# Order of the squared states between ScalarE and TensorE in a Mamba + MoE kernel: by batch, or by row

## What is computed

```
def step(h, inp):
    dA_t, dB_t, x_t, C_t, t = inp
    h = h * dA_t + dB_t * x_t[:, :, None]
    nrm = jnp.sqrt(jnp.sum(h * h, axis=(1, 2), keepdims=True))
    fac = jnp.minimum(20.0 / (nrm + 1e-08), 1.0)
    h = jnp.where(t % 10 == 0, h * fac, h)
    y = jnp.einsum('bdn,bn->bd', h, C_t) + D_param * x_t
    return (h, y)
```

## Time and profile before

| | us |
|---|---|
| runs of the kernel before | 733.01, 736.2, 736.84 |
| median of them | 736.2 |
| span of the profiled execution | 732.8 |
| PE / PE weight loads busy | 610.7 / 475.9 |
| DVE / ACT / POOL busy | 579.2 / 581.7 / 591.9 |
| segments run from | about 36 to 600 |

### The profile page before, as it was taken

How to read it: one execution, slowest core, us unless ns; L and a number is a source line. 1 busy time by engine, 2 the same in 40 slices (tenths; PEclk the granted TensorE clock), 3 DMA queues, 4 the chain that set the end, 5 groups by cost and what they waited for, 6 DMA issues and landing times.

```text
span 732.8 us, 12812 instructions
## 1 busy us (share of the span) xinstructions
PE 610.7 (83%) x3988; PEld 475.9 (65%) x3988; DVE 579.2 (79%) x918; ACT 581.7 (79%) x1218; POOL 591.9 (81%) x567
## 2 busy tenths in 40 slices
PE   6698989889979889998988999898878794289774
PEld 4346667757757667766766766776667783179764
DVE  5577799899889989998998999889898982843221
ACT  4899989999998999999999999999988731233330
POOL 4488889999998989999998999998798860177774
PEclk9889899999989999999999999999988887589998
DMA  5341423245145313614542271244215202147561
GB/s 159 117 157 36 146 80 117 62 143 162 61 145 144 127 63 100 202 61 133 156 127 63 85 210 64 105 139 133 64 66 175 66 18 73 47 129 207 167 182 48
DMA packets 61735, 83.17 MB, mean 114 GB/s; under 512 B 14998, under 2 KB 47544, under 8 KB 61672
## 3 DMA queue, kind: packets, MB, share of 16 engines
q1 hardware_dynamic: 57896, 76.07, 34.0%
q0 software_dynamic: 2560, 6.08, 3.0%
q10 hardware_dynamic: 1216, 0.27, 0.2%
HBM read 69.81 MB, written 12.80 MB: 113 GB/s over the span
## 4 chain that ended last, share of the span: by engine, by line
ACT 27%; PE 22%; issue 17%; POOL 15%; DVE 13%; DMA 4%; POOLq 0%; SPq 0%; DVEq 0%; ACTq 0%
ACT z L1098 9%; POOL h L855 8%; DVE h L1367 7%; PE ps L1725 7%; ACT ps L989 7%; POOL h L869 4%; PE ps L1617 4%; DMA z<-rows_d,gidx 3%; PE ps L588 2%; PE ps L601 2%; ACT L1059 2%; ACT dtb L1059 1%; ACT xx L1016 1%; PE ps L1699 1%; ACT L1098 1%
## 5 line engine op out<-in xcount | busy, mean ns | idle before, releaser
L1367 DVE TENSOR_TENSOR_SCAN h<-ps,h 128x902 f32<-128x902 f32 x204 | 320.4, 1610 | 33.5 <-ACT ps L989 23.6
L855 POOL TENSOR_TENSOR h<-u,scr 128x640 f32<-128x640 f32 x208 | 298.2, 1462 | 2.4
L1725 PEld LDWEIGHTS ps<-h,ident 128*128 128x128 f32 x1632 | 239.4, 199 | 24.2 <-issue 21.8
L1725 PE MATMUL ps<-h,ident 128*128 128x160 f32 x1632 | 243.9, 310 | 3.3 <-issue 3.3
L1098 ACT ACTIVATE z<-dtb,asc 128x240 f32<-128x240 f32 x576 | 237.4, 485 | 0.3
L989 ACT ACTIVATE ps<-z 128x820 f32<-128x820 f32 (+1 forms) x208 | 138.2, 689 | 16.0 <-DVE h L1367 8.9
L869 POOL TENSOR_TENSOR h<-h,scr 128x960 f32<-128x960 f32 (+1 forms) x52 | 106.0, 2038 | 1.1 <-DVE h L1383 1.1
L1418 DVE TENSOR_TENSOR h<-h,ps 128x640 f32<-128x640 f32 (+2 forms) x169 | 106.5, 642 | 0.2
L1617 PE MATMUL ps<-xnT,wT 128*128 128x488 f32 x144 | 77.2, 652 | 0.3 <-ACT xnT L974 0.3
L1699 PE MATMUL ps<-sqb,sel 128*8 128x32 f32 x832 | 33.6, 195 | 37.6 <-ACT sqb L999 27.7
L1699 PEld LDWEIGHTS ps<-sqb,sel 128*8 128x8 f32 x832 | 27.2, 91 | 53.0 <-ACT sqb L999 45.7
(11 more groups left out here) (193 smaller groups left out, 820.2 us busy)
## 6 DMA issues: line engine op xcount, KB each, us to landing
scr<-b_d SPq DMA_DIRECT2D x52, 640.0 KB, 4.6
scr<-c_d SPq DMA_DIRECT2D x52, 240.0 KB, 4.4
z<-in_L_ffn_w_dram SPq DMA_DIRECT2D x32, 256.0 KB, 3.1
cdg<-cdg_d SPq DMA_DIRECT2D x52, 93.8 KB, 2.1
xx_d<-xx SPq DMA_DIRECT2D x8, 256.0 KB, 2.0
xxr<-xx_d SPq DMA_DIRECT2D x8, 256.0 KB, 2.8
rows_d<-h2b SPq DMA_DIRECT2D x16, 120.0 KB, 2.0
rows_d<-xxr SPq DMA_DIRECT2D x16, 120.0 KB, 2.3
```

The lines of the kernel that those rows point to most:

```text
L855: pool.tensor_tensor(o.rearrange("p (n b) t -> p n b t", b=B), us.unsqueeze(1).to_broadcast([P, nn, B, SEG]), bb[:, S % RING, n0 * BS:(n0 ...
L1367: dve.tensor_tensor_scan(hs, region(G)[:, 0:(r1 - r0) * SLOT], hs, 0.0, ALU.mult, ALU.add).then_inc(gscan, 1)
L1725: pe.matmul(ps[:, YB, 0:H * BS], ident[:], hr[:, :, n * B:(n + 1) * B, 0:SEG], start=(n == 0), stop=False)
```

## The change

The squares are written in the order of the rows, so that the output of ACT (and of DVE in the one operation ahead of the first segment) is contiguous; PE then takes a batch's 32 values with a stride of eight, 32 bytes apart. No instruction is added, removed or moved on any engine; only the addresses of three kinds of operation differ.

```diff
+        sq_b = sqb[:].rearrange("p (r b) -> p b r", b=B)
...
                 r0, r1 = ((0, SQROW), (SQROW, ROWS))[part]
-                act.activation(sqb[:].rearrange("p (b r) -> p r b", b=B)[:, r0 // B:r1 // B, :],
-                               rows(h, S % RING)[:, r0:r1, SEG].rearrange("p (r b) -> p r b", b=B),
+                act.activation(sqb[:, r0:r1], rows(h, S % RING)[:, r0:r1, SEG],
                                ACT.Square).then_inc(sq_done, 1)
...
-            dve.tensor_tensor(sqb[:].rearrange("p (b r) -> p r b", b=B), h_first.rearrange("p (r b) -> p r b", b=B),
-                              h_first.rearrange("p (r b) -> p r b", b=B), ALU.mult).then_inc(sq_done, 1)
+            dve.tensor_tensor(sqb[:], h_first, h_first, ALU.mult).then_inc(sq_done, 1)
...
                 for b in range(B):
-                    ins = pe.matmul(ps[0:B, YB, NCOL:NCOL + H * NST], sel[:, b, :], sqb[:, b * H * NST:(b + 1) * H * NST],
+                    ins = pe.matmul(ps[0:B, YB, NCOL:NCOL + H * NST], sel[:, b, :], sq_b[:, b, :],
                                     start=(b == 0), stop=(b == B - 1))
```

## The result

The changed kernel takes 746.1 us (744.28 to 747.95, four runs) against 735.11 us (733.01 to 736.84, four runs): ratio 1.0158, 95% interval 1.0123 to 1.0194. It is slower by 11.0 us, 1.6%. The profiled execution took 745.95 us, with a span of 744.2 us against 732.8.

What follows compares the result with a forecast made beforehand. No engine bounds the span; the norm chain ends last at a segment's end. PE's 0.43 us a norm, less covers, gives 1.26 us a window, 10.5 in all, other terms 0: 736.2 to 746.7 us, range 733.5 to 751.

Steps and rivals of the forecast that it cites:

- The bound: At each segment's end, PE's norm chain ends last by 0.10 us, so time added to PE delays DVE's reduction.
- (a): ACT's squares: contiguous output with input still strided changes nothing; taken as 0, at most 0.05 us a segment.
- The argument from DVE: DVE's squares: strided input alone costs 2.06 ns a value, both sides 1.90, contiguous runs 1.06; strided output adds nothing.
- (c): PE's norm, 16 matmuls reading values 32 bytes apart: 0.43 us more a segment, between 0 and 0.62.
- The factor of two: PE's columns in the norm: a strided value doubles the price, as on ACT and DVE, 0.85 ns extra.
- The covers: Waits behind the norm, DVE's for ACT's decays and POOL's late start, absorb part; 1.26 us a six-segment window is paid.
- The waits of 0.35 and 0.36 us: DVE's scans waiting for ACT's decays behind two norms of a window; they leave 0.08 and 0.07 us of 0.43 paid.
- The sum: Whole kernel: 1.26 us a window over 8.3 windows, 10.5 us more, median 736.2 to 746.7; chance 0.46.
- PE's cadence hides the stride: Rival on PE's norm: the 0.85 ns float32 column hides the stride; 734.5 to 736.2 us, chance 0.39.
- A partial price: Rival on PE's norm: 0.1 to 0.3 us a norm; at 0.3, 6 us more, 742; chance 0.08.
- DVE's full price: Rival on PE's norm: 0.62 us a norm, 18.3 us more, 754.5; chance 0.04.
- the output was ACT's cost: Rival on ACT's squares: contiguous output shortens them to 376 and 238 ns; at most 1.7 us gained; chance 0.03, including anything faster.

Runs made afterwards that it cites:

- bf16_rows: Changed kernel with squares in bf16, in the order of the rows, PE's stride of eight being 16 bytes; 743.84 us against 734.19 (ratio 1.0129).
- stride three: Kernel before, PE taking its 32 values with a stride of three (12 bytes); one run, 748.5 us, where the kernel before took 750.17 us.
- stride four: Kernel before, PE taking its 32 values with a stride of four (16 bytes), each on its own line; ratio 1.0155.
- act_only: Changed kernel with PE's line put back to reading neighbours, leaving the output order alone; 732.54 us against 734.32 (ratio 0.9979).

## Why the prediction was right, point by point

- **The bound** was read rightly: the norm chain ended last by a tenth of a microsecond, and DVE's stand before `take_norm` rose from 0.10 to 0.58 us, by PE's extra time. That not all of it is paid had been said too; how much is absorbed is where the sizes went wrong.
- **(a)** Taken at 0, right within 10 and 2 ns an operation. The argument from DVE (a strided input alone doubles the price) was tested on ACT: input alone 574, output alone 574, both 584, neither 372 ns. I had drawn the value of neither at 376.
- **(c)** Sized at 0.43 us a norm, it is 0.49. The factor of two was the right form only by accident of the numbers. The runs show a pace of about one line in 1.8 ns, not a doubled column: bf16 columns, at half the price, are slowed to the same 58 ns. By the doubling, bf16_rows would have shown 27 ns. The bf16 rows from which I concluded that 1.68 ns might be enough for a line gave nearly the right number, but slightly too low; a line needs 1.8.
- **The covers.** That waits behind the norm absorb a part was right: the 1.65 us wait took all of it (the segment stays at 11.25 us). The other sizes were off. In the window from 249.52 us before and 251.05 after, the six segments, norm to norm, are longer by 0.34, 0, 0, 0.01, 0.28 and 0.30 us, 0.93 in all. The forecast was 1.26; with its covers and the 0.49 us of a norm it would have been 1.56.
  - *POOL covered nothing.* Where I had taken off 0.18 us, DVE's `restart` starts 2.03 us after the reduction in both kernels. POOL takes the norm up earlier in the changed kernel, after 0.26 us instead of 0.44, but its next operation is 0.19 us longer.

```profile
314.77 0.85 POOL L887 TENSOR_TENSOR fac<-nrm,neghalf_e 8x1 f32<-8x1 f32 x1
...
316.10 0.62 DVE L1341 SCALAR_TENSOR_TENSOR h<-ps,h 128x256 f32<-128x256 f32 x1
```

```profile
316.79 0.18 POOL L887 TENSOR_TENSOR nrm<-s,guard 8x1 f32<-8x1 f32 x1
317.05 1.04 POOL L889 TENSOR_TENSOR fac<-nrm,neghalf_e 8x1 f32<-8x1 f32 x1
...
318.56 0.62 DVE L1342 SCALAR_TENSOR_TENSOR h<-ps,h 128x256 f32<-128x256 f32 x1
```

  - *The waits of 0.35 and 0.36 us were worth 0.47.* Two scans of 2.04 and 1.18 us that follow each other without a wait take 3.10 to 3.14 us, since they overlap by about 0.1, and a wait takes that away as well. The fourth segment's scans ran from 350.11 to 356.75, 6.64 us, against 6.17 in the changed kernel.
  - *The scans that I took as free of waits were not.* They hid 0.13, 0.20 and 0.17 us inside a merged line of four scans, visible as 6.30, 6.37 and 6.34 us against 6.17.

  With these three the sum at 0.49 us is 0.36 + 0 + 0.02 + 0.02 + 0.29 + 0.32 = 1.01 us a window, near the 0.93 measured. At the 0.26 us of stride three it is 0.13 + 0 + 0 + 0 + 0.06 + 0.09 = 0.28, and 0.27 was measured; the forecast's covers would have charged 0.60.
- **The last eight segments.** I priced them like the others, at 8 x 0.21 = 1.7 us, and they cost 5.74. One of them has the wait for ACT described above and costs nothing; seven at 0.48 are 3.4 us. The remaining 2.4 us lie where the granted clock is low (0.86 between 500 and 600 us of the changed kernel, 0.90 before).

```profile
500.00:600.00 100.00, 86.62 (x543) 73.53 (x542) 84.73 (x110) 81.04 (x169) 81.24 (x71) 0.86 0.30 95
```

  DVE waits for PE's sum over the states there up to 1.83 us at a time. The kernel with doubled norms, with 0.90 in the same stretch, takes 91.97 us for its last eight segments, 3.84 more than before, and stride four takes 91.96. So most of the 2.4 us belongs to this execution's clock rather than to the norm's length.
- **The sum** of +10.5 us against +11.0 measured, and 746.7 us against 746.1, is therefore closer than its terms, and that closeness is luck: 6 x 1.26 = 7.6 us for six windows where 6.18 were paid, and 1.7 for the last eight segments where 5.74 were.
- **The rivals.** That PE's cadence hides the stride fell with the 59 ns. A partial price, 0.1 to 0.3 us a norm, fell with the 0.49 us. DVE's full price would have been 66 ns a matmul, 7 more than measured. That the output was ACT's cost fell with act_only and with the two runs on its input.

## What to carry to other kernels

When a layout has to be strided for somebody, ask which engine pays on the path between two serial steps: an engine whose other side is strided anyway, or which then waits, takes it for nothing, and one with nothing else to wait for pays it in full. Before a delay is spread over repeated segments, look at each kind of them for what covers it, the last ones too, and compare the length of merged lines between segments, since small waits hide inside. A shorter operation on PE is not a gain by itself where another engine is right behind it.

## What the runs showed of the hardware that I had not expected

- The values that PE streams past its weights go at 1.8 to 1.9 ns for each 16-byte line that they touch, in float32 and in bf16, at a granted clock of 1.00: 32 values in 30, 45, 58 and 59 ns at strides of 2, 3, 4 and 8 float32 values, and 58 ns for bf16 at 16 bytes.
- On ACT a strided input and a strided output are not added: 574, 574 and 584 ns for one, the other and both of 208 values, 372 for neither. The square costs 1.84 ns a value with the input 44 bytes apart and 2.35 with 352 bytes.
- A strided bf16 output (64 bytes apart) costs ACT 4.6 ns a value, against 1.8 for float32 (128 bytes apart).
- Two scans of DVE, 2.04 and 1.18 us long, take 3.10 to 3.14 us when they follow each other without a wait, so a short wait between them costs that much more than the view shows (0.47 us for one of 0.36).
- With bf16 squares, and half as many matmul instructions in the norm, two kernels were slower by 0.8% and 1.3%, at a mean granted clock lower by about 0.02; the cause of the lower clock is open.
